# A tower of token embedding, attention and experts: tokens in natural order, the last pair's expert stage as two units, waits reordered, all slot tables rewritten

## What is computed

```python
def tok(dayofweek, hour, month, dayofmonth, ...):          # Fourier features of four integer ids
    x = fourier_concat(...)                                # [16, 512, 24]
    h1 = relu(x @ W1 + b1)                                 # 128 wide
    h2 = h1 @ W2 + b2                                      # 64 wide
    return layernorm(h2) * gamma + beta + 0.1 * (x @ Wres + bres)

def attn(x, Wq, Wk, Wv, Wo):                               # 8 heads over one shared key/value of 64
    q = einsum('bsc,oc->bso', x, Wq).reshape(b, s, 8, 64).transpose(0, 2, 1, 3)
    k = einsum('bsc,oc->bos', x, Wk)
    v = einsum('bsc,oc->bos', x, Wv).reshape(b, s, 64)
    attn = softmax(einsum('bhsd,bdt->bhst', q, k) * scale)
    ctx = einsum('bhst,btd->bhsd', attn, v)
    return (ctx.transpose(0, 2, 1, 3).reshape(b, 512, s) projected by Wo)

def ffn(f, ...):                                           # 6 experts, the best 2 of each token
    p = softmax(relu(f @ router_w1 + b1) @ router_w2 + b2)
    w, i = top_k(p, 2); w = softmax(w)
    e = relu(f @ e1 + b1); e = relu(e @ e2 + b2); e = e @ e3 + b3      # all six, dense
    return sum over the two chosen experts of w * e

h = tok(ids); h = h + attn(layernorm(h)); h = h + ffn(layernorm(h))
```

## Time and profile before

| what | value |
|---|---|
| median of 3 runs | 669.76 us (667.29 to 671.34) |
| the profiled execution's own time | 672.91 us |
| its span | 671.1 us |
| TensorE matmuls busy | 644.7 us, 96% of the span |
| VectorE, ScalarE, GpSimd busy | 80%, 71%, 42% |

### The profile page before, as it was taken

The page is one execution under the profiler, slowest core; times in us unless marked ns, Lnnn a source line. Parts: engine busy times, 40 slices in busy tenths (PEclk is TensorE's granted clock), DMA queues, the critical chain, the costliest instruction groups (busy, mean ns, idle before and its releaser), DMA issues.

```text
span 671.1 us, 26756 instructions
## 1 busy us (share of the span) xinstructions
PE 644.7 (96%) x11632; PEld 360.9 (54%) x11632; DVE 539.1 (80%) x1068; ACT 476.0 (71%) x1193; POOL 279.7 (42%) x354
## 2 busy tenths in 40 slices
PE   7699999999999999999999999999999999999974
PEld 6345555555555466555655465555655555555653
DVE  4588678988788887989788887989889897977555
ACT  2388885887668866887668867697758875888331
POOL 1134112704763175622945156630947037311372
PEclk9799999999999999999999999999999999999978
DMA  4000000000000000000000000000000000000001
GB/s 173 1 2 2 2 2 3 2 2 2 19 4 2 2 3 19 3 2 2 4 19 2 2 3 20 2 2 3 3 19 2 2 3 19 2 2 2 4 2 32
DMA packets 9428, 6.66 MB, mean 10 GB/s; under 512 B 8672, under 2 KB 8672, under 8 KB 9184
## 3 DMA queue, kind: packets, MB, share of 16 engines
q1 hardware_dynamic: 9312, 4.97, 2.6%
HBM read 2.87 MB, written 2.10 MB: 7 GB/s over the span
## 4 chain that ended last, share of the span: by engine, by line
PE 90%; DVE 5%; ACT 2%; issue 1%; POOL 1%; DMA 1%; ACTq 0%; SPq 0%; DVEq 0%; POOLq 0%
PE s_bank L470 33%; PE s_bank L438 32%; PE s_bank L560 5%; PE s_bank L450 4%; PE s_bank L662 3%; PE s_bank L627 3%; PE s_bank L638 3%; PE s_bank L480 2%; ACT p L742 1%; PE s_bank L491 1%; PE s_bank L533 1%; PE s_bank L507 1%; PE s_bank L602 1%; PE s_bank L518 1%; POOL st L1177 1%
## 5 line engine op out<-in xcount | busy, mean ns | idle before, releaser
L742 ACT ACTIVATE p<-s_bank,nmax 128x512 f32<-128x512 f32 x512 | 347.3, 690 | 122.2 <-DVE nmax L868 121.7
L868 DVE TENSOR_REDUCE nmax<-s_bank 128x1 f32<-128x512 f32 x512 | 323.3, 681 | 36.2 <-PE s_bank L438 35.7
L438 PE MATMUL s_bank<-kf,g 64*64 64x512 f32 x2048 | 255.6, 597 | 1.1 <-DVE g L949 0.8
L470 PE MATMUL s_bank<-p,woz 64*64 64x256 f32 x4096 | 245.6, 378 | 1.8 <-ACT g L748 1.4
L470 PEld LDWEIGHTS s_bank<-p,woz 64*64 64x64 f32 x4096 | 153.6, 133 | 116.5 <-issue 37.6
L295 POOL TENSOR_TENSOR woz<-cst,rz 128x256 f32<-128x256 f32 x126 | 77.3, 634 | 246.9 <-DVE rz L874 246.9
L438 PEld LDWEIGHTS s_bank<-kf,g 64*64 64x64 f32 x2048 | 73.2, 134 | 91.2 <-issue 47.9
L742 ACT ACTIVATION_READ_ACCUMULATOR p<-s_bank,nmax 128x1 f32 x512 | 105.4, 206 | 0.0
L880 DVE STREAM_TRANSPOSE m<-s_bank 128x512 f32<-128x512 f32 x64 | 45.7, 714 | 24.5 <-PE s_bank L470 24.5
L1177 POOL TENSOR_TENSOR st<-st,power 128x8 f32<-128x8 f32 x24 | 39.5, 1644 | 37.7 <-DVE st L895 37.7
L304 POOL TENSOR_TENSOR y<-y,gt 128x768 f32<-128x768 f32 x28 | 41.3, 1475 | 17.6 <-DVE y L1094 17.6
(11 more groups left out here) (118 smaller groups left out, 504.4 us busy)
## 6 DMA issues: line engine op xcount, KB each, us to landing
tower_out<-o SPq DMA_DIRECT2D x16, 128.0 KB, 2.6
cst<-consts SPq DMA_DIRECT2D x1, 1070.0 KB, 8.5
e2t<-ids SPq DMA_DIRECT2D x1, 768.0 KB, 5.8
cst<-consts SPq DMA_DIRECT2D x1, 416.0 KB, 6.3
cst<-consts SPq DMA_DIRECT2D x1, 288.0 KB, 3.7
e2t<-ids SPq DMA_DIRECT2D x1, 256.0 KB, 3.5
cst<-consts SPq DMA_DIRECT2D x1, 3.0 KB, 1.8
```

The source lines that it names most:

```text
L438: last = pe.matmul(double[half(q), 512 * r:512 * r + 512], g[half(r), a // 2 % 2, a % 2, first:first + 64], kf[half(r), par, a // 4, :], s ...
L470: last = pe.matmul(bank("PV", i, a)[half(q), 512 * hh:512 * hh + 256], woz[half(r), kept, 2 * mm + hh, :], keys[:, q, :, :], start=(part = ...
L742: nc.scalar.activation(p[:, 8 * kept + c % 8, :], bank("S", i, c - r)[:, 512 * r:512 * r + 512], ACT.Exp, bias=nmax[:, c % 16:c % 16 + 1], ...
L868: nc.vector.tensor_reduce(nmax[:, c % 16:c % 16 + 1], bank("S", i, c - r)[:, 512 * r:512 * r + 512], AX.X, ALU.max, negate=True).then_inc( ...
```

## The change

1. The 1024 tokens of a pair lie in natural order: tiles 0 to 3 are the first sequence, 4 to 7 the second (before, each tile held 64 tokens of either). The host lays the ids out so; FIN, the copy of the keys, the logits, the stores and the tile indices follow. FIN now puts the two heads of a group (c) on the two column halves of the array, and takes the sequences one after the other: 128 matmuls of 128 columns for a pair in place of 64 of 256.
2. The last pair's expert stage is two units with their own semaphores and tables: tiles 0 to 5 (`L[0]`) and tiles 6 and 7 (`L[1]`, whose FIN is in two parts of one tile). Every step of ffn is issued for each of the two; each operation covers the unit's tiles alone. The shared buffers between the units and the pair before (`xt`, `rh`, `e1t`, `e2t`, `gt`) get waits on the pair before.
3. Where an instruction waits for two things, the wait that is met last is written last: in `exps`, `pv`, `turn` and FIN.
4. The stores of the last pair go out by sequence, each once its four tiles are summed.
5. All tables are new, and with them the ring. V of the first pair moves from slot 38 to slot 8. Of pair 6 (Z) the three E2 move from slots 63, 63, 65 to 23, 45, 49, and the four Y from 69, 77, 97, 98 to 62, 66, 84, 90. In F the gating is drawn together from slots 32 to 52 to slots 37 to 45.

The diff, cut to what the prediction speaks of:

```diff
-V_FIRST, V_FIRST_ACT = 38, 37
+V_FIRST, V_FIRST_ACT = 8, 7
...
+LAST_PARTS = ((0, 6), (6, 7, 8))
...
+UNITS = tuple((i, (0, 8), F) for i in range(PAIRS - 2)) + ((PAIRS - 2, (0, 8), Z),) + tuple(
+    (PAIRS - 1, parts, f) for parts, f in zip(LAST_PARTS, L))
...
+            def store(i, b2):
+                dst = out[2 * i + b2, :, :].rearrange("(t q) c -> q t c", q=128)
+                sp.dma_start(dst, o[:, 4 * b2:4 * b2 + 4, :]).then_inc(stored, 16)
...
+            for b2 in range(2):
+                sp.wait_ge(y_pool, units[PAIRS - 1].pool0 + (b2 + 1) * W_LAST)
+                sp.wait_ge(y_dve, 2 * (b2 + 1))
+                store(PAIRS - 1, b2)
...
+            def value_products(u, t0, t1):
+
+                par = u.i % 2
+                for b2 in range(2):
+                    lo, hi = max(t0, 4 * b2), min(t1, 4 * b2 + 4)
+                    if lo >= hi:
+                        continue
+                    for n in range(8):
+                        for g4 in range(4):
+                            q, s2 = g4 // 2, g4 % 2
+                            for c in range(2):
+                                last = pe.matmul(
+                                    bank("FIN", u.u, s2)[half(c), 512 * q + 32 * lo:512 * q + 32 * hi],
+                                    v[quarter(g4), par, b2, n, :],
+                                    m[quarter(g4), b2, 2 * (lo - 4 * b2) + c:2 * (hi - 4 * b2):2, n, :],
+                                    start=(n == 0), stop=(n == 7), skip_group_check=True)
                 return last
...
             def exps(i, c):
                 a, r = c // 8, c % 2
+                wait(act, pvd, HH * i + a - KEPT + 1)
                 act.wait_ge(maxed, SLOTS * i + c + 1)
-
-                wait(act, pvd, HH * i + a - KEPT + 1)
...
+                if slot == f["T"]:
+                    if u is units[-1]:
+                        pe.wait_ge(u.norm.sums, 1)
...
-    t = t.reshape(n, PAIRS, 2, HEADS, KD).transpose(0, 1, 3, 2, 4).reshape(n, PAIRS, QUARTERS, QT).transpose(2, 0, 1, 3)
+    t = t.reshape(n, PAIRS, QUARTERS, QT).transpose(2, 0, 1, 3)
```

More of the change, by code:

```diff
@@ L2 @@
 from contextlib import ExitStack
+from dataclasses import dataclass
 import numpy as np
@@ L179, in ring_places, with last, tiles, cols @@
     return place
+@dataclass
+class Norm:
+    xc: object
+    sq: object
+    st: object
+    sums: object
+    steps: object
+    squared: object
+    n: int
+    count: int
+    tiles: slice
+@dataclass
+class Unit:
+    u: int
+    i: int
+    parts: tuple
+    f: dict
+    n: int
+    pool0: int
+    dve0: int
+    norm: Norm
+    fin_ps: object
+    hatt_sb: object
+    x2t_ps: object
+    xt_sb: object
+    rh_ps: object
+    rh_sb: object
+    l_ps: object
+    gate: object
+    gate_act: object
+    gated: object
+    e1_ps: object
+    e1_sb: object
+    e2_ps: object
+    e2_sb: object
+    y_ps: object
+    y_sb: object
+    @property
+    def last(self):
+        return self.i == PAIRS - 1
+    @property
+    def tiles(self):
+        return slice(self.parts[0], self.parts[-1])
+    @property
+    def cols(self):
+        return slice(64 * self.parts[0], 64 * self.parts[-1])
+    @property
+    def js(self):
+        return range(self.parts[0] // 2, self.parts[-1] // 2)
 def tower(nc, ids, consts, out):
```

706 lines of the change are left out of this document (372 added, 334 removed), and 16 rows, old and new, of tables (F, L, Z).

## The result

The changed kernel takes 686.21 us, the median of 4 runs (683.83 to 689.17), against 669.44 for the kernel before. The ratio is 1.0242, with a 95% interval of 1.020 to 1.028. The forecast was 661.4 in a range of 656.5 to 668.0, with 0.76 for faster. So the sign is wrong and the time lies far outside the range. The profiled execution took 683.83, its span is 681.9. That is 10.8 more than before's 671.1.

The account below looks back on a forecast made before the run. TensorE, busy 96%, bounds the middle; chains of small operations bound the tail. End = 620.06 + 2.6 + 41.4 - 0.5 - 0.8 = 662.7 against 671.1, 8.4 less, so median 669.76 becomes about 661.4 us, range 656.5 to 668.

Parts of the forecast that it names:

- The step that failed: FIN in the middle: 128 matmuls of 128 columns for 64 of 256, within 0.15 us a pair, taken as zero.
- the row of Y: Profile row for one Y on TensorE: 48 instructions in 0.70 us, 14.6 ns each, used to price FIN's smaller matmuls.
- Rival C: FIN in the middle: fixed time per matmul whatever its columns, 3.6 us more a pair, 17 slower, 687; chance 0.02.
- Its milder form: FIN in the middle: about 25 ns floor between small matmuls' starts, 2.8 us more a pair, 681; no separate chance.
- The waits: Reordered waits in the middle: priced at nothing, shortening a wait on ScalarE, which is busy 71% and off the chain.
- The tail: From the last score tile's end to the span's end: 51.0 us before, forecast 41.4, less 0.8 for small operations.
- T: End of the last score tile: 620.06 us in the profile before, forecast to move to 622.6.
- the 7.4 us for the layer norm of six tiles: VectorE's layer norm in the tail: 8.9 us for eight tiles before, 7.4 for six with a Y in between.
- The forecast's own test: On the tail: the forecast is wrong at its root if the tail is shortened by less than 5 us.
- Rival A: VectorE becomes the bound in the middle, around the gating; at 2 us a pair 3.6 slower, 673.5; chance 0.12.
- Rival B: The tail gives less: TensorE at 1.2 GHz or FIN's small parts doubled; gain 2.5 to 6, 664 to 667; chance 0.20.
- V to slot 8: First pair's V fills TensorE's 1.42 us idle time ahead of the first product: gain 0 to 0.9, taken as 0.5.

## Why the prediction was wrong

**The step that failed** is FIN: "Either way it is within 0.15 us for a pair, 1 us over seven; I take zero." It is 1.87 us for a pair, 13.1 over seven, and some 5 more in the tail (8.85 us against 3.62 with half the instructions). The rate of starts was right: the first 152 matmuls of a FIN start within 2.2 us, 14.4 ns each, against 14.6 from the row of Y; a FIN without its hole is 3.9, and that is 2.0 of the 13.1. What was wrong is that Y's 48 matmuls in a row say how fast TensorE starts what it has, and not how long that lasts. With their loads they are 96 instructions. FIN has 512 with its loads, and past what is in store TensorE gets 256 in 3.45 us, 27 ns for a matmul with its load.

**Rival C** had the direction, at 0.02: FIN of 5 us or more. Its mechanism, a fixed time for each matmul, is not what happens; the matmuls run at 14 ns until the store is empty. Its milder form, by the Trainium skill, page "TensorE: Matmul & The Clock Gate", section "Back-to-back issue gap", gave 681. The section states its floor of about 25 ns for 1 to 64 columns, and the traces contradict it: 128 matmuls of 32 columns in the changed kernel's tail start within 1.4 us (653.58 to 655.00), 11 ns each, and FIN's with 128 columns follow at 14.4 ns. That the 27 ns of a starved TensorE lie near 25 is a nearness of numbers; what TensorE waits for there is its next instructions. That 681 came nearer than 661.4 is luck in the same way.

**The waits**: "The reordered waits I also price at nothing". They cost 3.3 to 3.8 us in the three kernels on which they were tried, 2.5 to 2.8 of it between the first and the seventh FIN. A rival for them was missing.

**The tail, apart from this, was right.** Without FIN's extra instructions it is 41.5 us; the forecast was 41.4 less 0.8 for small operations. VectorE's additions for six tiles start at T + 5.5 (forecast 5.1), those for two at T + 14.6 (14.4). With the holes they start at T + 7.8 and T + 20.2, and the tail is 47.0. One term was right by luck: the 7.4 us for the layer norm of six tiles is less than its own parts give (three quarters of 7.3, the power's 1.65 and a Y of 0.95 make 8.1), and measured without the holes it is 7.5 (630.07 to XT at 637.57). The forecast's own test, "wrong at its root if the tail is shortened by less than 5 us", came true with 4.0, by FIN again.

**The sum.** With before's number of instructions in FIN and before's order of waits, all else of the change being in, the kernel takes 662.13 us; the forecast was 661.4. From there to the changed kernel it is 3.8 for the waits and 20.3 for FIN: 13.1 in the seven FINs, 5.5 in the tail, and 1.7 that no row was named for. (The two profiled executions differ by less, 15.9: the changed kernel's reached its first FIN 2.9 us earlier than the other's, with the same head.)

**Rival A** did not happen: in the run with half the instructions VectorE keeps the pair at 77.54 us, and with the old order of waits at 77.16. VectorE matters in another way, which I had not foreseen: where FIN ends late, its additions hold up the maxima behind them, and score tiles wait. As far as the traces show, this is what ate the gain when FIN was cut in two. **Rival B** is not what shortened the gain: without the extra instructions the tail comes out as forecast. Only behind the holes did TensorE run slower, 1.56 us for a Y of 48 matmuls (646.32 above) against 0.91: from 646.3 to 649.0 the granted clock is 0.50, the lower level of 1.2 GHz, and 1.00 at the same place with half the instructions. **V to slot 8** is within what can't be measured.

No kernel that computes everything beat the kernel before. The natural order pays 20 us for 7 us of gain (with the waits in their old order) as long as FIN needs twice the matmuls for it; a natural order for the last pair alone, with FIN of before in the middle, was not tried.

## To carry to other kernels

Count TensorE's instructions, weight loads too, in every dense stretch, not its columns alone. Here 190 to 500 instructions of a FIN went at 14 ns a matmul, and beyond them supply gave 256 in 3.45 us; a change that halves the matmuls' size to please a layout has to be priced by that. An idle time marked "issue" within one group of equal matmuls is the sign to look for, even where it occurs once. And price a reordering of waits by running it alone: an order that only looks better cost half a per cent here.

## What the hardware showed that was not expected

- TensorE's holes in FIN stand at fixed places in its program, 193 recorded instructions into blocks of 256, in every trace here that has one, and move when instructions are added ahead: by 64 matmuls for 64. Each ends 1.2 to 1.6 us behind the landing of a 16384-byte packet of the instruction queue.
- A starved TensorE gets one block in 3.42 to 3.47 us (346.68 to 350.13, 286.83 to 290.29, 641.88 to 645.30 above), between some pairs of holes in 3.7 to 4.0, while 128 matmuls of 128 columns with their loads, one block, start within 1.8 us.
- The granted clock was 1.00 in the 13 us ahead of a FIN of 12.5 us with three holes, 0.67 in it, and 0.94 in the 14 us behind.
- 64 small matmuls of 8 columns with weights of 128x128 took 13.8 us at the start of the program, 0.22 us each at a granted clock of 1.00, with nobody waited for.
- Two waits ahead of one instruction, both met in the end, were not free to swap: in four places together 3.3 us for the kernel before, ratio 1.0044 with its interval above 1.
